# W times y for the batch statistics as three fp32r products instead of one in fp32

## The reference

```
x   = x + ref(gn(x))
g   = g_w v + g_b                          # 128 channels x 4096
f   = v^T v                                # 4096 x 4096
y   = softmax(f, last axis) g^T            # 4096 x 128
wy  = W_w y^T + W_b                        # 256 x 4096
wy  = batchnorm(wy) over all images and places, gamma, beta
ref = wy + v
```

## Time and profile before

| | before |
|---|---|
| median of 3 runs | 2054.38 us |
| profiled execution, its own time | 2054.48 us |
| its span, first to last instruction | 2052.8 us |
| TensorE matmuls busy | 2006.7 us, 98% |
| VectorE busy | 1545.2 us, 75% |
| ScalarE busy | 1157.2 us, 56% |
| GpSimd busy | 888.3 us, 43% |
| DMA | 299.94 MB, mean 146 GB/s |

### The profile page before, as it was taken

One profiled execution on the slowest core, in us unless ns is written; L12 is line 12 of the kernel. 1 busy time (PEld: TensorE's weight loads), 2 busy tenths in 40 slices (PEclk: granted clock), 3 DMA queues, 4 the chain that ended last, 5 costly groups with the idle time before them and its releaser, 6 DMA issues.

```text
span 2052.8 us, 28691 instructions
## 1 busy us (share of the span) xinstructions
PE 2006.7 (98%) x9428; PEld 1466.5 (71%) x9428; DVE 1545.2 (75%) x3116; ACT 1157.2 (56%) x2391; POOL 888.3 (43%) x688
## 2 busy tenths in 40 slices
PE   5999999999999999999999999999999999999999
PEld 4787777766688777776678777776668877777444
DVE  6777777877777777797777777787777777777777
ACT  4345556666444546667554555666644454666657
POOL 3011224779602124678821122567960202467740
PEclk9999999999999999999999999999999999999999
DMA  3222333556511332565622233465651132245998
GB/s 138 106 90 79 121 108 125 190 180 196 167 68 67 129 103 93 173 209 158 215 85 85 77 108 119 128 191 167 196 181 67 67 123 94 92 143 187 354 336 328
DMA packets 107507, 299.94 MB, mean 146 GB/s; under 512 B 11488, under 2 KB 11872, under 8 KB 93536
## 3 DMA queue, kind: packets, MB, share of 16 engines
q1 hardware_dynamic: 107360, 298.11, 43.0%
HBM read 157.55 MB, written 140.51 MB: 145 GB/s over the span
## 4 chain that ended last, share of the span: by engine, by line
PE 86%; ACT 4%; DVE 4%; issue 3%; POOL 3%; DMA 1%; SPq 0%; DVEq 0%; ACTq 0%; POOLq 0%
PE bank L1412 15%; PE bank L1333 12%; PE bank L1335 12%; PE bank L1334 12%; PE bank L1384 9%; PE bank L1423 5%; PE bank L1416 5%; PE bank L1417 5%; PE bank L1576 3%; PE bank L1487 2%; ACT ring L905 1%; DVE bank L1155 1%; ACT phi L946 1%; PE bank L1340 1%; PE bank L1368 1%
## 5 line engine op out<-in xcount | busy, mean ns | idle before, releaser
L946 ACT CAST phi<-bank 128x512 fp32r<-128x512 f32 x480 | 280.8, 585 | 594.9 <-PE bank L1384 594.4
L1109 DVE TENSOR_SCALAR_CACHE_REDUCE ring<-bank 128x512 f32<-128x512 f32 x560 | 386.1, 689 | 242.2 <-PE bank L1335 190.7
L1333 PE MATMUL bank<-xh 128*128 128x512 f32 (+3 forms) x1152 | 508.7, 442 | 4.0 <-POOL xl L785 3.6
L1140 DVE TENSOR_TENSOR plo<-bank,phi 128x512 fp32r<-128x512 f32 x480 | 329.6, 687 | 141.3 <-ACT phi L946 111.2
L1335 PE MATMUL bank<-xh,xl 128*128 128x512 f32 (+3 forms) x1152 | 435.2, 378 | 0.0
L1334 PE MATMUL bank<-xl,xh 128*128 128x512 f32 (+3 forms) x1152 | 433.0, 376 | 0.0
L905 ACT ACTIVATE ring<-ring,nmax 128x512 f32<-128x512 f32 x464 | 334.5, 722 | 1.0
L1384 PEld LDWEIGHTS bank<-ident,ring 128*128 128x128 f32 x1856 | 223.4, 140 | 120.2 <-issue 61.3
L825 POOL TENSOR_TENSOR fy_d<-fy_d,maxrow 128x512 f32<-128x512 f32 x173 | 224.3, 1300 | 183.7 <-DMA fy_d<-spill 183.7
L825 POOL TENSOR_TENSOR fy_c<-fy_c,maxrow 128x512 f32<-128x512 f32 x193 | 249.6, 1297 | 107.3 <-DMA fy_c<-spill 107.2
L1384 PE MATMUL bank<-ident,ring 128*128 128x128 f32 x1856 | 279.7, 273 | 10.2 <-DVE plo L1140 8.0
(11 more groups left out here) (165 smaller groups left out, 2933.2 us busy)
## 6 DMA issues: line engine op xcount, KB each, us to landing
spill<-ring SPq DMA_DIRECT2D x108, 1024.0 KB, 4.4
fy_c<-spill SPq DMA_DIRECT2D x200, 256.0 KB, 4.1
fy_d<-spill SPq DMA_DIRECT2D x180, 256.0 KB, 4.1
ring<-x_dram SPq DMA_DIRECT2D x42, 512.0 KB, 5.8
lbuf<-spill SPq DMA_DIRECT2D x68, 256.0 KB, 5.0
yd<-yn SPq DMA_DIRECT2D x24, 256.0 KB, 3.4
out_dram<-ring SPq DMA_DIRECT2D x10, 512.0 KB, 3.4
fx_a<-x_dram SPq DMA_DIRECT2D x8, 512.0 KB, 7.2
```

The lines of the kernel that those rows point to most:

```text
L1109: last = nc.vector.tensor_scalar(slot_tile(u, t), src, 1.0, None, ALU.mult, ALU.max, accum_out=rowm[:, t, c:c + 1])
L1140: nc.vector.tensor_tensor(plo[:, n % LOS, :], whole(p), phi[:, HI_BUF[n], :].bitcast(F32), ALU.subtract).then_inc(lo_made, 1)
L1333: nc.tensor.matmul(dst, xh[:, k, rows], xh[:, k, cols], start=(k == 0), stop=False)
```

## The change

- W is brought as two halves in fp32r (`wws`: high by ScalarE, low by GpSimd, at the start). The fp32 W lies in `lsb` at first, as `ww_raw`, and is loaded again in the last image at step 160 (WW_BACK) into the place of g's weights, for the fp32 products that remain (`wwt`).
- y gets a high half (`make_yh`, ScalarE, cast at step 4) and a low half (`make_yl`, into `lsb_r`): VectorE at step 5 for blocks 4 and 5 of the first three images; GpSimd for all others of them and for blocks 0 to 3 of the last image, ahead of the first left tile beyond step 10 of the block that follows (`YL_AT`: steps 14, 13, 12, 12 for blocks 0 to 3 and 11 for block 6), and for block 7 at the head of the next image.
- `project` is then three fp32r products, W high and low times y high, W high times y low; only the third waits for y's low half. Blocks 4 to 7 of the last image stay fp32.
- The first projection moves from step 5 to step 6, its count with it from 7 to 8.
- y lies in `colmax` for blocks 0 to 6 of every image. So ScalarE's next take no longer waits for the store; VectorE waits for store and low half before it writes `colmax` (or `bst`, now in `colmax` too) for the next image. `yn` holds the high half, `maxrow` that of block 7, `lsb` the low half; ScalarE waits for the projections before it reuses them.

```diff
 assert max(NEXT_PRODUCTS) + 1 < TILES + FIRST_EXP
-INVERT_AT, TAKE_AT, SCALE_AT, WY_AT = 0, 1, 2, (5, 9)
+INVERT_AT, TAKE_AT, SCALE_AT, WY_AT = 0, 1, 2, (6, 9)
 LATE = [1] * NB
...
              for j in range(1, NB)}
...
+YL_BY_POOL = [(b, j) for b in range(B) for j in range(NB) if j < 4 or (j > 5 and b < B - 1)]
+YL_BY_DVE = [(b, j) for b in range(B - 1) for j in (4, 5)]
+HALVED = sorted(YL_BY_POOL + YL_BY_DVE)
+YL_AT = {j: min(w for w, p in enumerate(LEFT) if p > (j + 1) * TPB + SCALE_AT + LATE[j] + 7) for j in range(NB - 1)}
+WW_BACK = 5 * TPB
+assert WW_BACK > max(G_AT) + 2
+YL_OF = {w: j for j, w in YL_AT.items()}
...
-            return colmax[:, j, :] if b == B - 1 and j < NB - 1 else yn[:, :]
+            return colmax[:, j, :] if j < NB - 1 else yn[:, :]
...
+        def yh_home(j):
...
+            return (yn_r if j < NB - 1 else maxrow_r)[:, :]
...
+        def wait_yl(eng, b, j):
...
+            if (b, j) in YL_BY_POOL:
+                eng.wait_ge(yl_made, YL_BY_POOL.index((b, j)) + 1)
+            elif (b, j) in YL_BY_DVE:
+                eng.wait_ge(yl_made_v, YL_BY_DVE.index((b, j)) + 1)
...
                 sp.wait_ge(y_made, b * NB + j + 1)
-                sp.dma_start(yd[bass.ds(b, 1), :, j * W:(j + 1) * W].rearrange("b p w -> p (b w)"), yn[:, :]
+                sp.dma_start(yd[bass.ds(b, 1), :, j * W:(j + 1) * W].rearrange("b p w -> p (b w)"), y_home(b, j)
                              ).then_inc(y_stored, 16)
...
                     store_y(b - 1, NB - 1)
+                if not more and s == WW_BACK:
+                    sp.wait_ge(g_made, B * (2 * NB))
+                    sp.dma_start(wwt, ww).then_inc(ww_back, 16)
                 if not more and s in FIN_AT:
...
+            def make_yl(b, j):
...
+                pool.wait_ge(yh_made, HALVED.index((b, j)) + 1)
+                if b + j > 0:
+                    pool.wait_ge(left_summed, b * (NB - 1) + j)
+                nc.gpsimd.tensor_tensor(lsb_r[:, :], y_home(b, j), yh_home(j).bitcast(F32), ALU.subtract
+                                        ).then_inc(yl_made, 1)
...
             def image(b, more):
+                if b > 0:
+                    make_yl(b - 1, NB - 1)
                 for c in range(len(NEXT_G), NB):
...
                 for w in range(NLEFT):
+                    if w in YL_OF and (b, YL_OF[w]) in YL_BY_POOL:
+                        make_yl(b, YL_OF[w])
                     if more and w == AHEAD[GROUP_AT + 4]:
...
                 make_gl(0, c)
+            pool.wait_ge(ww_hi, 1)
+            nc.gpsimd.tensor_tensor(wws[:, 1, :], ww_raw, wws[:, 0, :].bitcast(F32), ALU.subtract).then_inc(ww_lo, 1)
             for b in range(B - 1):
...
                     act.wait_ge(left_sub_v, sum(v < LEFT_OF[j][0] for v in VSUBS))
+                if j == 1:
+                    act.wait_ge(wy_made, b * (K * NB))
                 nc.scalar.copy(maxrow[:, :], sps).then_inc(maxrow_made, 1)
...
                 act.wait_ge(left_added, b * NLEFT + LEFT_OF[j][-1] + 1)
+                act.wait_ge(wy_made, b * (K * NB) + K * j)
                 nc.scalar.copy(lsb[:, :], lacc).then_inc(left_taken, 1)
...
                 if j > 0:
-                    if b == B - 1:
+                    act.wait_ge(wy_made, b * (K * NB) + K * j)
+                    if (b, j - 1) not in HALVED:
                         act.wait_ge(y_made, b * NB + j)
-                    else:
-                        act.wait_ge(wy_made, b * (K * NB) + K * j)
-                        act.wait_ge(y_stored, b * (16 * NB) + 16 * j)
                 nc.scalar.copy(yn[:, :], sps).then_inc(inverse_taken, 1)
...
+            def make_yh(b, j):
...
+                act.wait_ge(y_made, b * NB + j + 1)
+                if j == NB - 1:
+                    act.wait_ge(left_sub, pool_subs(b + 1, 0))
+                nc.scalar.copy(yh_home(j), y_home(b, j)).then_inc(yh_made, 1)
...
                     take_inverse(b - 1, NB - 1)
+                if j >= 1 and i == SCALE_AT + LATE[j - 1] + 1 and (b, j - 1) in HALVED:
+                    make_yh(b, j - 1)
+                if tail and s == SCALE_AT + 2:
+                    make_yh(b - 1, NB - 1)
                 if tail and s == HEAD - 1:
...
                 make_xh(0, c, first=True)
+            nc.scalar.copy(wws[:, 0, :], ww_raw).then_inc(ww_hi, 1)
             for s in range(FIRST_EXP, 0):
...
                 dve.wait_ge(x_in[c], n * 16 + 16)
+                if n > 0 and c == 0:
...
+                    dve.wait_ge(y_stored, (n - 1) * (16 * NB) + 16)
+                    wait_yl(dve, n - 1, 0)
                 for k in range(K):
...
                         dve.wait_ge(f_taken, n * NPROD + s)
+                    if n > 0 and j == 0 and t == 1:
...
+                        dve.wait_ge(y_stored, (n - 1) * (16 * NB) + 16 * c)
+                        wait_yl(dve, n - 1, c - 1)
                     before = slot_tile(u, 0) if j == 0 and t == 1 else cm
...
                 nc.vector.tensor_tensor(y_home(b, j), yps[:, j % 2, :], yn[:, :], ALU.mult).then_inc(y_made, 1)
...
+            def make_yl(b, j):
...
+                dve.wait_ge(yh_made, HALVED.index((b, j)) + 1)
+                dve.wait_ge(left_summed, b * (NB - 1) + j)
+                nc.vector.tensor_tensor(lsb_r[:, :], y_home(b, j), yh_home(j).bitcast(F32), ALU.subtract
+                                        ).then_inc(yl_made_v, 1)
...
                     add_g(b + 1, *NEXT_G_AT[p - 1])
+                if j >= 1 and i == SCALE_AT + LATE[j - 1] + 2 and (b, j - 1) in YL_BY_DVE:
+                    make_yl(b, j - 1)
                 if j >= 1 and i - 2 in WY_AT:
...
-                pe.wait_ge(y_made, b * NB + j + 1)
+                rows = slice(h * P, (h + 1) * P)
                 shared_free(b, "wy", j, h)
-                nc.tensor.matmul(sps, wwt[:, h * P:(h + 1) * P], y_home(b, j), start=True, stop=True
+                if (b, j) not in HALVED:
+                    pe.wait_ge(ww_back, 16)
+                    pe.wait_ge(y_made, b * NB + j + 1)
+                    nc.tensor.matmul(sps, wwt[:, rows], y_home(b, j), start=True, stop=True).then_inc(wy_made, 1)
+                    return
+                if b + j == 0:
+                    pe.wait_ge(ww_lo, 1)
+                pe.wait_ge(yh_made, HALVED.index((b, j)) + 1)
+                nc.tensor.matmul(sps, wws[:, 0, rows], yh_home(j), start=True, stop=False)
+                nc.tensor.matmul(sps, wws[:, 1, rows], yh_home(j), start=False, stop=False)
+                wait_yl(pe, b, j)
+                nc.tensor.matmul(sps, wws[:, 0, rows], lsb_r[:, :], start=False, stop=True
                                  ).then_inc(wy_made, 1)
...
             for k in range(K):
-                last = nc.tensor.matmul(lacc[:, 2 * k:2 * k + 2], wwt[:, k * P:(k + 1) * P], bgc[:, :],
+                last = nc.tensor.matmul(lacc[:, 2 * k:2 * k + 2], ww_raw[:, k * P:(k + 1) * P], bgc[:, :],
                                         start=True, stop=True)
...
+            pe.wait_ge(ww_back, 16)
...
             def final_wy(u, parts):
```

More of the change, by code:

```diff
@@ L460, in nonlocal_block @@
             plo = scoped("plo", [P, LOS, W])
+            yn_r = scoped("yn_r", [P, W])
+            maxrow_r = scoped("maxrow_r", [P, W])
+            lsb_r = scoped("lsb_r", [P, W])
+            wgs = scoped("wgs", [P, K, 2 * CI])
         fx_a = sb("fx_a", [P, K, N])
@@ L465, in nonlocal_block @@
         keep = sb("keep", [P, HIS + LOS, W])
+        yn = sb("yn", [P, W])
+        maxrow = sb("maxrow", [P, W])
+        lsb = sb("lsb", [P, W])
+        wwb = sb("wwb", [P, 2, C])
+        wwt = wwb[:, 0, :]
         ring = sb("ring", [P, SLOTS - 1, T, W])
@@ L493, in nonlocal_block @@
         lbuf = sb("lbuf", [P, LBUFS, W])
-        lsb = sb("lsb", [P, W])
-        maxrow = sb("maxrow", [P, W])
-        yn = sb("yn", [P, W])
         ident = sb("ident", [P, P])
         gavg = sb("gavg", [P, P])
-        wgs = sb("wgs", [P, K, 2 * CI], F32R)
         wgh, wgl = wgs[:, :, 0:CI], wgs[:, :, CI:2 * CI]
-        wwt = sb("wwt", [P, C])
+        wws = sb("wws", [P, 2, C], F32R)
+        ww_raw = lsb[:, 0:C]
         bgc = sb("bgc", [P, 2])
@@ L504, in nonlocal_block @@
         vecs = sb("vecs", [P, 3, K])
-        bst = sb("bst", [P, K, NB, 6])
+        bst = colmax[:, 0, 0:K * NB * 6].rearrange("p (k c s) -> p k c s", k=K, c=NB)
         mv = sb("mv", [P, K, 2])
@@ L532, in nonlocal_block @@
         consts_in = sem("consts_in")
+        ww_back = sem("ww_back")
         consts_made = sem("consts_made")
@@ L584, in nonlocal_block @@
         y_stored = sem("y_stored")
+        ww_hi = sem("ww_hi")
+        ww_lo = sem("ww_lo")
+        yh_made = sem("yh_made")
+        yl_made = sem("yl_made")
+        yl_made_v = sem("yl_made_v")
         wy_made = sem("wy_made")
@@ L745, in _ @@
             sp.dma_start(wraw, wg.rearrange("(k p) c -> p k c", p=P)).then_inc(consts_in, 16)
-            sp.dma_start(wwt[:, :], ww).then_inc(consts_in, 16)
```

(1 more changed line is left out.)

## The result

The changed kernel takes 2072.89 us (median of 5 runs, 2070.45 to 2074.44), against 2054.38 before: ratio 1.0088, 95% interval 1.0078 to 1.0099, slower by 0.9%. The forecast was 2062, slower by 0.35%; its sign was right, its size less than half. The time lies above the range of 2050 to 2069.

A forecast was written before the change was run, and what follows sets the result against it. TensorE, busy 98% of the span, was taken as the bound; -6.3 + 6.4 + 2.0 + 6.3 + 0.4 = +8.8 us, less 1.6 of idle time, gave +7.2 on 2054.5: forecast 2062 us, range 2050 to 2069.

The forecast's parts named there:

- idle time used up: TensorE's idle gaps, 1.3 us an image, absorb some of its delays; 0.4 of it taken, 1.6 us in all.
- The low half on VectorE: Block 5: making y's low half on VectorE was priced at 1.1 us, delaying the count of the first projection.
- the move of the projection: First projection from step 5 to 6, count 7 to 8; matters only where something else wants the shared bank at step 7.
- block 5, image 4: Last image's block 5: no low half made there, only the move of the count acts; +0.4 us, bounds 0 and 1.3.
- The products: Three fp32r products replace one fp32 projection; 45 of 56 projections gain 0.14 us each on average, 6.3 us.
- Block 3: TensorE's third product waits 1.8 us for GpSimd's low half of y; +1.6 us, 6.4 over four images.
- Block 4: GpSimd's low half of y makes tile 7's third product wait; +0.5 us, 2.0 over four images, bounds 0.2 and 0.9.
- Block 5: Column turning waits for VectorE's later count behind y's low half; +2.1 us, 6.3 over three images, bounds 1.7 and 2.7.
- Block 6: VectorE's low half comes in time; waits taken as 0, bounds 0 and 1 us per image for the other blocks.
- Last image, blocks 6 and 7: Projections there stay fp32; no delay was expected, taken as 0.
- Rival 4: Block 5's half on VectorE costs only a PSUM operand's price, 1.2 us less: 2060.5; 0.61 together with the forecast.
- Rival 3: GpSimd's queue becomes the bound in blocks 5 to 7, 2 to 3 us more per image: 2071; chance 0.09.

The follow-up runs named there:

- y in PSUM: Changed kernel, but y of blocks 2, 4, 5 scaled in PSUM and VectorE's low half read there, first projections at step 5 except blocks 3, 4, 6; 2051.85 us, ratio 0.9982.
- the copy's run: Changed kernel, but VectorE's low half of y (blocks 4 and 5) is a copy of y to fp32r instead of a subtraction; 2071.31 us, ratio 1.0075.

## Why the prediction was right in sign and wrong in size

The prediction's sum was +8.8, less 1.6 of idle time used up: +7.2. The profiled execution has +16.0. Four steps failed, and they make most of the 8.8 us between. The low half on VectorE was priced at 1.1 us and took 1.74 to 1.79 in block 5 (2.4 us in sum); in block 6 the same instruction was put at nothing (2.5, with the gain of the products that didn't show there); idle time was taken as given back and was not (1.6); the move of the projection was put at nothing in the last image's blocks 6 and 7 (0.9). Term by term, over all images:

| term | predicted | measured |
|---|---|---|
| blocks 0, 1, 2, 7 (block 7 without image 4) | -3.9 | -4.1 |
| block 3 | +5.8 | +6.0 |
| block 4 | +1.4 | +1.9 |
| block 5, images 1 to 3 | +5.9 | +8.3 |
| block 5, image 4 | +0.4 | +0.4 |
| block 6, images 1 to 3 | -0.8 | +1.7 |
| blocks 6 and 7, image 4 | 0 | +0.9 |
| idle time used up | -1.6 | 0 |
| start (+0.7), and the rest | 0 | +0.9 |
| sum | +7.2 | +16.0 |

- **The products: right.** Without the low half, and with the move's share taken off, all 56 gain 7.2 us, 0.13 each where 0.14 was said. Blocks 1 to 4 gain 0.31 to 0.35 for both projections in every image, so 0.16 to 0.18 each, as the pitch in the earlier trace rows had it; the other blocks differ by image (block 0 gains 0, 0.6 and 0.4, block 6 nothing). By the four passes that the Trainium skill gives true FP32 ("FP8 and Floating Point Precision", section "TensorE Precision Notes"), with one for the reduced form, which is a reading of that section and not its words, it would have been 0.21 each. The runs have less.
- **Block 3: right in place, order and size** (a hole of 1.69 against 1.8). GpSimd's queue was read step by step from the earlier trace rows. **Block 4: right, a little small.**
- **Block 5: the mis-sized term is the low half on VectorE.** The move was given 1.0 of the 2.1 (912.01 less 911.04) and costs 1.12 alone. The low half was given 1.1 as the middle of the earlier trace rows and lasts 1.79 in the second image, 1.74 to 1.79 in the three. The rows held the answer: their spread of 0.68 to 1.67 is not scatter. In the trace of before, 14 of the 15 subtractions of L1162 end 0.54 to 0.59 us after the instruction that GpSimd had under way as they began, and the fifteenth, 0.68 us long, met GpSimd idle. One of them, with GpSimd's two beside it, then the place in block 5 where the low half was to go (VectorE's and GpSimd's):
```profile
1931.24 0.80 DVE L1162 TENSOR_TENSOR fy_d<-fy_d,maxrow 128x512 f32<-128x512 f32 x1
1930.22 1.29 POOL L825 TENSOR_TENSOR fy_c<-fy_c,maxrow 128x512 f32<-128x512 f32 x1
1931.45 1.73 POOL L825 TENSOR_TENSOR fy_d<-fy_d,maxrow 128x512 f32<-128x512 f32 x1
...
905.73 0.69 DVE L1155 TENSOR_TENSOR bank<-ring,bank 128x512 f32<-128x512 f32 x1
906.46 1.28 POOL L825 TENSOR_TENSOR fy_c<-fy_c,maxrow 128x512 f32<-128x512 f32 x1
```
A subtraction that begins at 906.50, 0.08 behind the addition as in the changed kernel, would end 0.55 after 907.74, so it would take 1.8. Reading the pairs in the two timelines, not the middle of a group, would have given it, if narrowly: begun 0.05 earlier it would have met the instruction ahead. Three times 0.7 is 2.1 of the 2.4 missed; 0.1 an image more is the move. That tile 6 waits first was not in the working; it costs nothing of its own, because the turning two steps on waits for the same queue. The rule cited from the Trainium skill ("GPSIMD Engine Reference", section "Specifications") pointed the right way: taking the second SBUF operand away brought the half to 0.69. But the one-operand copy waits too. Beside instructions with two SBUF inputs, the same row of that page names VectorE instructions in a 2-port performance mode, which the prediction's sentence left out. Whether the copy ran in such a mode, no run here shows; its 0.28 us behind GpSimd is well below the 0.67 and more of the subtractions that didn't wait.
- **Block 6: taken as 0, and wrong.** "In time" was so, but VectorE's instruction of 1.20 to 2.46 us delays VectorE's and GpSimd's queues in a full stretch: +0.39, +0.45 and +0.81 where a gain of 0.28 was due. With the half from PSUM, or with none, it is 0: so the half is 0.4 to 0.8 of it, and the gain of the products doesn't show here even without it, for a reason that stays open.
- **Last image, blocks 6 and 7: the move, taken as 0 outside block 5.** In the kernel before it costs 1.6 in block 6 and gives back 0.3 in block 7; taken out of the kernel with y in PSUM it gives 2.0 and costs 0.5.
- **Idle time: nothing was given back.** The windows show after with the old idle time, all but 0.1 us of it, plus the holes; that 0.1, in block 3, was counted in that block's term already. (The 1.3 us were those of three blocks, and taken for an image.) Those gaps wait for what TensorE itself releases, which the prediction said and then took 1.6 off all the same.
- **The median lies 2.4 above the profiled execution**, which no term had. The four others ran at a mean clock of 0.997 to 0.999, the profiled ones of before and after at 1.000. The four profiled executions of experiments with a mean clock of 0.998 or 0.999 show falls of 3.4 us behind idle time of TensorE, and one costs 1.6 us (block 3 of the last image +3.07 instead of +1.5 in the copy's run). By these traces 0.999 goes with one fall and 0.998 with two or three, so a few such falls in the holes that the change makes would be the 2.4, or more. That is argued, not shown: no trace of a run of the changed kernel at that clock is there.

Rival 4 (the low half at the price of a PSUM operand) is what y in PSUM brought about, and its price came out: 0.69 us. No rival was as dear as the truth. Rival 3 named GpSimd's queue in blocks 5 to 7 and a subtraction stretched by VectorE's reads; its mechanism does act in block 6, at 0.4 to 0.8 an image where it had 2 to 3, but it was held for unlikely and kept apart from the forecast, where both hold at once. That its 2071 is the nearest number to the measured one is luck.

## What to carry to other kernels

Where a group's durations spread by more than a factor of two, look at what the neighbour engine does at each start before taking the middle. An instruction added to a full queue can cost its length at the waits behind it, so for each place in GpSimd's or VectorE's list ask which of the two neighbours TensorE wants first: one place was worth 1.9 us an image here. When one operand of VectorE's subtraction can stay in PSUM, its time no longer hangs on GpSimd (0.69 us instead of 1.20 to 2.46 here).

## What the runs showed of the hardware

**VectorE and GpSimd take turns.** A subtraction of VectorE with both operands in SBUF, begun while GpSimd runs, ends 0.55 us after GpSimd's running instruction, and GpSimd's next one takes 1.72 to 1.78 us instead of 1.29. Its own length is 0.68 with GpSimd idle. VectorE's copy from SBUF to SBUF waits likewise, and ends 0.28 behind. With one operand in PSUM the subtraction took 0.68 to 0.69 in all 16 cases of two runs, each beside a busy GpSimd. By tile in the changed kernel:
```profile
L1260 DVE TENSOR_TENSOR lsb_r<-colmax,yn_r x6: 1203/1766/2464, 420.0 to 1459.7; 128x512 fp32r<-128x512 f32 x6
```
**It can lose its turn.** The 2464 waited for two instructions of GpSimd, and four low halves (three in one execution, one in another) waited for 12 or more of them, 18 us, until the queue had a gap. They end 0.55 after the last of them. All four are in block 6, and it differs between executions of one kernel.

**TensorE's clock.** After TensorE stood idle for about 2 us in a full stretch the granted clock fell from 1.00 to 0.50 for 3.4 us in some places: behind the 2.1 us hole in block 5 in all three images of one kernel and in one of three of another, behind the 1.7 us in block 3 in two profiled images and not in the others, and in the last image behind two idle stretches of 1.1 and 1.3 us close together, in two kernels. In the profiled execution of the changed kernel no hole brought one. Where one did, the hole in block 3 or 5 cost 1.6 us more than its length. In the four stalls of 18 us TensorE was idle for 15 us, the clock was at 0.50 for 17.1 us (20.5 in one), and 5 to 8 of these came after work was back.
